# The last two tiles of a mixture-of-experts stage reach their tokens through PSUM

## The reference

```
gate_logits = einsum('bsd,de->bse', x, gate_kernel)          # 8 experts
top_k_weights, top_k_indices = top_k(gate_logits, 2)
top_k_weights = softmax(top_k_weights)
h0 = einsum('bsd,edm->bsem', x, w0)                           # 256 -> 512
h1 = einsum('bsd,edm->bsem', x, w1)
inter = silu(h0) * h1
out = einsum('bse,bsem,emd->bsd', combine, inter, wo)         # 512 -> 256
x = x + out
```

## Time and profile before

| | |
|---|---|
| median of 3 runs | 536.52 us (533.1 to 539.55) |
| profiled execution, its own time | 537.06 us |
| its span | 534.8 us |
| mean granted TensorE clock | 0.963 |
| busy in the span | PE 92%, DVE 64%, ACT 60%, POOL 25% |
| expert tiles in the span | about 404 to 519 us |
| after the last reduction | about 519 to 534.8 us |

### The profile page before, as it was taken

The page is one execution under the profiler, slowest core; times in us unless marked ns, Lnnn a source line. Parts: engine busy times, 40 slices in busy tenths (PEclk is TensorE's granted clock), DMA queues, the critical chain, the costliest instruction groups (busy, mean ns, idle before and its releaser), DMA issues. The chain is left out here.

```text
span 534.8 us, 11854 instructions
## 1 busy us (share of the span) xinstructions
PE 491.5 (92%) x4181; PEld 418.1 (78%) x4190; DVE 343.3 (64%) x743; ACT 318.4 (60%) x759; POOL 134.3 (25%) x150
## 2 busy tenths in 40 slices
PE   8899999999999999999999879999849999999970
PEld 3778888888898888888779857777637888888860
DVE  6666666667644676666558465678674667666754
ACT  4677777778526777777673267898313444544430
POOL 5710000012100000000000189996122433443220
PEclk9999999999999999999999997999859999999995
DMA  9521111211100112210000243441044555554527
GB/s 263 182 61 60 59 59 59 59 54 46 29 31 21 45 57 59 59 59 20 1 1 2 68 131 119 130 149 42 1 157 150 153 162 174 164 143 165 167 69 245
DMA packets 25043, 49.10 MB, mean 92 GB/s; under 512 B 2977, under 2 KB 12210, under 8 KB 25010
## 3 DMA queue, kind: packets, MB, share of 16 engines
q1 hardware_dynamic: 20434, 40.65, 25.0%
q0 software_dynamic: 2240, 6.04, 3.3%
q10 hardware_dynamic: 2336, 1.97, 1.2%
HBM read 42.48 MB, written 6.16 MB: 91 GB/s over the span
## 5 line engine op out<-in xcount | busy, mean ns | idle before, releaser
L717 PE MATMUL psum<-a_xt_hi,a_qk_hi 128*128 128x512 f32 x128 | 53.7, 420 | 0.9 <-POOL a_qk_lo L325 0.9
L629 DVE COPY a_weights_t<-psum 64x256 f32<-64x256 f32 x32 | 13.7, 428 | 60.7 <-PE psum L834 60.7
L717 PE MATMUL psum<-a_xt_hi,a_qk_lo 128*128 128x512 f32 x128 | 50.1, 392 | 0.0
L1066 ACT ACTIVATE x_probs<-psum,x_neg_max 128x128 f32<-128x128 f32 x128 | 45.8, 401 | 7.1 <-DVE x_neg_max L1124 7.1
L717 PE MATMUL psum<-a_xt_lo,a_qk_hi 128*128 128x512 f32 x128 | 50.0, 390 | 0.0
L1558 ACT ACTIVATE e_inner_hi<-psum 128x512 fp32r<-128x512 f32 x23 | 13.8, 598 | 56.4 <-PE psum L1734 56.4
L1002 POOL MEMSET x_v_pad<- 128x1024 f32 x1 | 1.0, 952 | 167.5 <-POOLq L262 167.5
L1723 PE MATMUL psum<-expert_w_hi,e_x_hi 128*128 x92 | 38.4, 418 | 1.2 <-ACT e_x_hi L1538 1.2
L1515 POOL DMA_INDIRECT picks_dram<-x_wout,e_pick_row x23 | 22.7, 987 | 62.6 <-DVE x_wout L1671 62.6
L1663 DVE TENSOR_TENSOR e_inner_lo<-psum,e_inner_hi 128x512 fp32r<-128x512 f32 x23 | 15.9, 692 | 34.6 <-ACT e_inner_hi L1558 34.6
L848 PE MATMUL psum<-a_weights_t,a_v 64*128 64x64 f32 x256 | 34.9, 276 | 3.5 <-issue 2.6
(11 more groups left out here) (235 smaller groups left out, 1497.6 us busy)
## 6 DMA issues: line engine op xcount, KB each, us to landing
x_k_t<-in_expert_wo SPq DMA_DIRECT2D x23, 512.0 KB, 3.8
a_qk_raw<-in_wqk SPq DMA_DIRECT2D x32, 256.0 KB, 2.6
x_xn_t<-in_expert_w SPq DMA_DIRECT2D x13, 512.0 KB, 3.8
a_wv_raw<-in_wv SPq DMA_DIRECT2D x17, 256.0 KB, 2.8
xn_dram<-xn SPq DMA_DIRECT2D x2, 1024.0 KB
x_probs_t<-in_expert_w SPq DMA_DIRECT2D x3, 512.0 KB, 3.8
x_sb<-in_x SPq DMA_DIRECT2D x2, 512.0 KB, 4.8
x_k_t<-in_wo SPq DMA_DIRECT2D x1, 1024.0 KB, 10.4
```

Source lines behind the costliest of these rows:

```text
L717: last = pe.matmul(out, pick_l(left[a], k), pick_r(right[b], k), start=start and n == 0, stop=n == 3 * KD - 1, skip_group_check=not start)
L1066: last = act.activation(probs[:, ch, place, :], s_ps[ch][:, place, :], ACT.Exp, bias=neg_max[:, ch, place:place + 1], accum_out=sums[:, b ...
```

## The change

Only tiles 0 to 20 are stored to `picks_dram` as before. Rows of tiles 21 and 22 (`LATE = 2`) stay in SBUF, scaled by their picks' shares, and are multiplied on PE with one-hot matrices that place each row at its token. For every batch b of 128 tokens one PSUM region `late_ps[b]` gathers tile 21's product, tile 22's product, and the rows of the first picks, scaled on ACT and added by a product with the identity. DVE adds the rows of the second picks to x by a multiply-add, and at the end the PSUM region.

What that needs beforehand: rows of `picks_dram` that tiles 21 and 22 would have written are filled with zeros (`clear_late`, POOL at tile 4). The shares are written to DRAM element by element (`store_shares`, SP at tile 1) and gathered by slot (`fetch_shares`, POOL at tile 5). The token of each late slot is worked out (`late_tokens`, POOL at tile 5), and the one-hot matrices are made by 8 compares each (`make_hot`, POOL at tiles 6 and 7). The result copies of tiles 20, 21 and 22 move from DVE to ACT (`last_rows`). Reads of `picks_dram` are issued by SP alone, in transfers of two batches, those of the second picks first; those of the first picks wait until the `wo` buffer they go into is free. Some routing tiles move into the unused `c.v`, which changes no instruction.

```diff
@@ constants
+LATE = 2
+STORED = TILES - LATE
+READ_ORDER = (4, 6, 0, 2)
+TOKEN_ORDER = (4, 5, 6, 7, 0, 1, 2, 3)
+AHEAD = 3
...
-    picked = [c.v, c.k_t[:, :, :].rearrange("p k n -> p (k n)").rearrange("p (b d) -> p b d", b=B)]
+    picked = [c.k_t[:, :, :].rearrange("p k n -> p (k n)").rearrange("p (b d) -> p b d", b=B), c.v]
+    hot = [row_hot[:, :, :].rearrange("p n r -> p (n r)").bitcast(F32), sb("e_late_hot", [P, B * P], F32)[:, :]]
+    hot = [t.rearrange("p (b t) -> p b t", b=B) for t in hot]
+    zeros = c.x_mask[:, :, :].rearrange("p a s -> p (a s)").bitcast(F32)
...
+    late_ps = [c.bank[i][:, h * D:(h + 1) * D] for i in (6, 7, 0, 3) for h in range(2)]
@@ SP
+                if left == TILES - 2:
+                    store_shares()
+            def store_shares():
+                sp.wait_ge(picks_known, 1)
+                sp.dma_start(share_dram[0:1, :], ones_f[0:1, 0:1]).then_inc(share_stored, 16)
+                sp.dma_start(share_dram[1:1 + PICKS * P, :].rearrange("(n p) d -> p n d", p=P),
+                             share[:, :, :].rearrange("p k b -> p (k b)").unsqueeze(2),
+                             allow_slow_non_contiguous=True).then_inc(share_stored, 16)
...
+            sp.wait_ge(late_cleared, 16 * LATE)
             for slot in range(2):
-                sp.wait_ge(y_stored[slot], 16 * ((TILES + 1 - slot) // 2))
-            for b in range(B):
-                sp.dma_start(picked[0][:, b, :], picks[0, :, b, :]).then_inc(gathered[b], 16)
-            for b in range(0, B, 2):
-                sp.wait_ge(mixed, TOPK * b + 3)
-                sp.dma_start(out[b], c.x_sb[:, b, :]).then_inc(out_stored, 16)
+                sp.wait_ge(y_stored[slot], 16 * ((STORED + 1 - slot) // 2))
+            for k in (1, 0):
+                for b in READ_ORDER:
+                    if k == 0:
+                        sp.wait_ge(wo_lo_ready, TILES if b < HB else TILES - 1)
+                    sp.dma_start(picked[k][:, b:b + 2, :], picks[k, :, b:b + 2, :]).then_inc(gathered[k][b // 2], 16)
+            for n in range(0, B, 2):
+                sp.wait_ge(finished, n + 1)
+                sp.dma_start(out[TOKEN_ORDER[n]], c.x_sb[:, TOKEN_ORDER[n], :]).then_inc(out_stored, 16)
@@ POOL
+            def clear_late():
+                pool.memset(zeros, 0.0).then_inc(zeroed, 1)
+                pool.wait_ge(zeroed, 1)
+                for tile in range(STORED, TILES):
+                    pool.indirect_dma_start(out=picks_dram, out_offset=bass.IndirectOffsetOnAxis(ap=pick_row[:, tile:tile + 1], axis=0),
+                                            in_=zeros, in_offset=None).then_inc(late_cleared, 16)
+            def fetch_shares():
+                pool.wait_ge(share_stored, 32)
+                for i in range(LATE):
+                    pool.indirect_dma_start(out=late_share[:, i:i + 1], out_offset=None, in_=share_dram,
+                                            in_offset=bass.IndirectOffsetOnAxis(ap=token_row[:, STORED + i:STORED + i + 1], axis=0)
+                                            ).then_inc(share_known, 16)
+            def late_tokens():
...
+            def make_hot(i):
+                for b in range(B):
+                    last = pool.tensor_scalar(hot[i][:, b, :], iota[:, 0:P], late_at[:, i, b:b + 1], None, ALU.is_equal)
+                last.then_inc(hot_made, 1)
...
                 if tile > 1:
                     store(tile - 2)
-            store(TILES - 2)
-            store(TILES - 1)
+                if tile == 4:
+                    clear_late()
+                elif tile == 5:
+                    fetch_shares()
+                    late_tokens()
+                elif 6 <= tile < 6 + LATE:
+                    make_hot(tile - 6)
@@ ACT
+                if not more(left, LATE + 1):
+                    last_rows(tile, slot, pair)
+            def last_rows(tile, slot, pair):
+                act.wait_ge(y_done, tile + 1)
+                act.wait_ge(y_stored[slot], pair * 16)
+                if tile < STORED:
+                    act.activation(y_rows[:, slot, :], y_ps[slot], ACT.Copy).then_inc(y_ready, 1)
+                else:
+                    act.wait_ge(share_known, 16 * LATE)
+                    at = tile - STORED
+                    act.activation(y_rows[:, slot, :], y_ps[slot], ACT.Copy, scale=late_share[:, at:at + 1]).then_inc(late_ready, 1)
...
-            for b in range(B):
-                act.dma_start(picked[1][:, b, :], picks[1, :, b, :]).then_inc(gathered[b], 16)
+            for n, b in enumerate(TOKEN_ORDER):
+                act.wait_ge(gathered[0][b // 2], 16)
+                act.activation(picked[0][:, b, :], picked[0][:, b, :], ACT.Copy, scale=share[:, 0, b:b + 1]).then_inc(scaled, 1)
@@ DVE
-                dve.wait_ge(y_done, tile + 1)
-                wait_past(dve, y_stored[slot], pair * 16)
-                dve.tensor_copy(y_rows[:, slot, :], y_ps[slot]).then_inc(y_ready, 1)
+                if more(left, LATE + 1):
+                    dve.wait_ge(y_done, tile + 1)
+                    wait_past(dve, y_stored[slot], pair * 16)
+                    dve.tensor_copy(y_rows[:, slot, :], y_ps[slot]).then_inc(y_ready, 1)
...
+            for b in TOKEN_ORDER:
+                dve.wait_ge(gathered[1][b // 2], 16)
+                dve.scalar_tensor_tensor(out=c.x_sb[:, b, :], in0=picked[1][:, b, :], scalar=share[:, 1, b:b + 1],
+                                         in1=c.x_sb[:, b, :], op0=ALU.mult, op1=ALU.add).then_inc(mixed, 1)
+            for n, b in enumerate(TOKEN_ORDER):
+                dve.wait_ge(mixed, n + 1)
+                dve.wait_ge(tokens_done, n // 2 * 2 + 2)
+                dve.tensor_tensor(c.x_sb[:, b, :], c.x_sb[:, b, :], late_ps[b], ALU.add).then_inc(finished, 1)
@@ PE
-                reduce(tile, slot, pair)
+                if left == 0:
+                    pe.wait_ge(late_ready, 1)
+                    pe.wait_ge(hot_made, LATE)
+                    for b in TOKEN_ORDER[:AHEAD]:
+                        to_tokens(b, 0)
+                reduce(tile, slot, pair, left)
+            def to_tokens(b, i):
+                pe.matmul(late_ps[b], hot[i][:, b, :], y_rows[:, (STORED + i) % 2, :], start=i == 0, stop=False, skip_group_check=True)
             tiles(pe, step)
+            for b in TOKEN_ORDER[AHEAD:]:
+                to_tokens(b, 0)
+            pe.wait_ge(late_ready, LATE)
+            for n, b in enumerate(TOKEN_ORDER):
+                to_tokens(b, 1)
+                pe.wait_ge(scaled, n + 1)
+                pe.matmul(late_ps[b], c.ident[:, :], picked[0][:, b, :], start=False, stop=True,
+                          skip_group_check=True).then_inc(tokens_done, 1)
```

More of the change, by code:

```diff
@@ L1368, with expert_phase @@
 TO_TILES = float(3 * P * 2 ** 22)
-def expert_phase(c, xn_dram, picks_dram, out):
+LATE = 2
[3 more added lines that the diff above has]
+AHEAD = 3
+def expert_phase(c, xn_dram, picks_dram, share_dram, out):
     nc = c.nc
@@ L1388, in expert_phase, with in_scratch @@
     chosen_id = sb("e_chosen_id", [P, B, TOPK], F32)
[L1389 removed]
+    scratch = c.v[:, :, :].rearrange("p b d -> p (b d)")
+    def in_scratch(at, n):
+        return scratch[:, at:at + n]
+    chosen = in_scratch(384, TOPK * B * NE).rearrange("p (k b e) -> p k b e", k=TOPK, b=B)
     either = sb("e_either", [P, B + 1, NE], BF16)
@@ L1398, in expert_phase @@
     base = sb("e_base", [P, NE], F32)
-    place = sb("e_place", [P, B, NE], F32)
-    place_k = sb("e_place_k", [P, TOPK, B, NE], F32)
+    place = in_scratch(576, B * NE).rearrange("p (b e) -> p b e", b=B)
+    place_k = in_scratch(640, TOPK * B * NE).rearrange("p (k b e) -> p k b e", k=TOPK, b=B)
     row_f = sb("e_row_f", [P, TOPK, B], F32)
-    reached = c.v[:, :, :].rearrange("p b d -> p (b d)")[:, 0:PICKS * TILES].rearrange("p (n t) -> p n t", n=PICKS)
+    reached = in_scratch(0, PICKS * TILES).rearrange("p (n t) -> p n t", n=PICKS)
     in_tile = sb("e_in_tile", [P, PICKS, TILES], F16)
@@ L1445, in expert_phase @@
     t_done, t_ready, t_lo_ready, y_done, y_ready = sem("e_t_done"), sem("e_t_ready"), sem("e_t_lo_ready"), sem("e_y_done"), sem("e_y_ready")
-    gathered = [sem(f"e_gathered{i}") for i in range(B)]
+    gathered = [[sem(f"e_gathered{k}_{b}") for b in range(0, B, 2)] for k in range(TOPK)]
     mixed, out_stored = sem("e_mixed"), sem("e_out_stored")
+    zeroed, late_cleared, late_chain, hot_made = sem("e_zeroed"), sem("e_late_cleared"), sem("e_late_chain"), sem("e_hot_made")
+    share_stored, share_known, late_ready = sem("e_share_stored"), sem("e_share_known"), sem("e_late_ready")
+    scaled, tokens_done, finished = sem("e_scaled"), sem("e_tokens_done"), sem("e_finished")
     def tiles(eng, step):
@@ L1516, in store @@
                                         in_=y_rows[:, slot, :], in_offset=None).then_inc(y_stored[slot], 16)
+            def clear_late():
[11 more added lines that the diff above has]
+            def late_tokens():
```

(20 more changed lines are left out.)

23 lines of the change are left out of this document (8 added, 15 removed).

## The result

The changed kernel is **slower by about 1.5%**. The first comparison gave 545.26 us against 538.86 for the kernel before on the same chip (ratio 1.0154, 95% interval 1.0118 to 1.019), a later one 545.05 against 537.35 (1.0171, 1.0113 to 1.0229); by the ratios that is 8.3 and 9.2 us. The prediction was 536.8, between 531.5 and 542.0, "the same" at 0.74. It was wrong.

What follows compares the result with a forecast made beforehand. TensorE was taken to bound the expert loop, a chain of waits the end. Tail -2.8, POOL's stall +2.0 and POOL beside VectorE +1.1 gave +0.3: 537.4 against 537.06, hence median 536.8 us, range 531.5 to 542.0.

Steps and rivals of the forecast that it cites:

- Share store on SP: 2048 four-byte packets ahead of tile 4's wo load on SP's queue: expected to cost nothing, upper end 3.4 us.
- cover of 5.35 us: Expert loop: lateness a POOL row load can have, beyond 3.6 us landing, before TensorE waits.
- Rival 4: Four-byte writes hold tile 4's weights: up to 3.4 us, replacing some of POOL's stall; 537.1 to 540.2 us; chance 0.06.
- the size of POOL's stall: TensorE's wait from POOL's added work at tiles 4 to 7: 3.1 us, bounds 0 and 9.7.
- load(10): POOL's row load for tile 10, behind both compare blocks: 7.4 us late, stopping TensorE for 2.0 us.
- load(9): POOL's row load for tile 9, behind the first eight compares, expected late through carried-over POOL work.
- 1.8 + 8c: Lateness of tile 9's row load: 1.8 us carried plus eight one-hot compares of c = 0.51 us each.
- the term for POOL beside VectorE: One-hot blocks meeting VectorE's wo_lo subtract lose 0.57 us a tile, 1.14 us for two.
- rival 3: VectorE's subtract and POOL's reads fully exclude each other: 2 x 1.23 us in place of 1.14; 538.1 us; chance 0.08.
- Rival 5: TensorE drops to clock 0.5 in the tail, costing 7.4 us: 544.2 us; chance 0.03.
- The tail: From tile 21's products to the end: TensorE's fp32 products at 0.442 us each set the pace; gain 2.8 us.
- The cover of 0.4 us for the first scaled rows: Tail: first-pick rows arrive some 0.4 us before TensorE's first pair needs them, so their reads were costed at nothing.

Runs made afterwards that it cites:

- either cure alone: Changed kernel with either the shares stored as 16 rows of 512 bytes (540.07 us, ratio 1.0065) or POOL's added work in smaller pieces (541.54 us, ratio 1.0081).

## Why the prediction was wrong

**The step that failed is "Share store on SP"**, in its sentence "I take 44 ns, the queue with the smaller packets: nothing; upper end 3.4". It priced the packets by their own time on the engines and looked for the harm in one place, the weights of tile 4. The packets were even cheaper than that, 9 ns. The cost came behind them: with 4-byte writes that share 64 bytes with their neighbours, the transfers under way (all of them touch DRAM) were slow for some 10 us, POOL's row loads among them, one of which landed 13.1 us after its issue in place of 3.6. By the prediction's cover of 5.35 us on top of 3.6 that is a stall of about 4; measured were 3.65 idle, and 3.9 us lost. Rival 4 named the same store, but with weights as the victim and at a price of 0 to 3.4; it also let POOL catch up meanwhile, so that its cost replaced the other stall. The two stalls lie four tiles apart and add up: either cure alone leaves 4.05 or 5.66 us of wait.

**The second step that failed is the size of POOL's stall:** 3.1 us were predicted, 4.55 idle and 6.9 lost. The mechanism was right, a load that POOL issues too late, but it came a load earlier than the sum has it. The sum puts the excess at load(10), behind sixteen compares, with load(9) late by 1.8 + 8c = 5.9 us, hardly more than the cover of 5.35. The run with the shares as 16 rows shows the lateness without the other stall: tile 6's load went out at 421.10, three steps of 4.87 later is 435.71, and load(9) went out at 445.19, 9.5 us late. That less 5.35 is 4.1; its wait was 4.05. While TensorE stood and then ran at half clock, POOL made the second eight compares, and tile 10 found its rows.

Two terms made most of the 3.6 us between 5.9 and 9.5. The compare was taken at 0.51 and took 0.59, 0.6 us for eight. And the term for POOL beside VectorE was too small: it counted the compares alone, at 0.57 a block, while in front of load(9) three of POOL's instructions met a subtract of wo_lo, and lost 0.9 (the second read of the shares), 0.7 (a store) and 0.7 us (a compare). The remaining 0.5 us lie in small operations and gaps. Full exclusion, rival 3 and the rule of the Trainium skill (SBUF — State Buffer, Who interferes with whom), is what these traces show: in every run each compare of more than 0.9 us, up to 1.69, overlapped a subtract and ended 0.38 to 0.48 us behind its end; where a compare went ahead, the subtract was longer (1.57 in place of 1.23 above). Only some 0.4 us at the seam overlapped freely. Rival 3 stood at 0.08, because the in_tile product's 1.72 us were read as a slowdown of less than half its overlap. VectorE's two compares beside it, taken one by one, read otherwise:

```profile
395.59 1.22 DVE L1618 TENSOR_TENSOR e_row_hot<-e_iota,e_at_row 128x1024 f16<-128x1024 f32 x1
...
396.73 1.83 DVE L1618 TENSOR_TENSOR e_row_hot<-e_iota,e_at_row 128x1024 f16<-128x1024 f32 x1
```

The product began at 395.75, within the first, and ended at 397.47, 0.66 us behind its end at 396.81; the second compare took 0.61 us longer than the first. Each of the two waited once for the other. Rival 3 priced the one-hot compares only, so its 1.3 us more are not what was lost here.

**A term was missing: the clock behind a stall.** The prediction counted a stall as its idle time. Behind the 4.55 us TensorE ran at 0.50 for 4.6 us, which made 6.85 of it. Rival 5 looked for the half clock in the tail, where it did not come.

**The tail was right:** 2.8 us predicted, 2.8 measured; 0.442 a product against 0.43. It was as predicted bound by TensorE, as the run without the identity products showed by gaining 1.6 us more there (15.7 to 14.1). The cover of 0.4 us for the first scaled rows, costed at nothing, was too thin in five of the ten other profiles, by 0.2 to 0.9 us.

**Sum:** -2.8 (predicted -2.8), +6.9 at tile 7 (predicted 3.1), +4.2 at tiles 2 and 3 (predicted 0; 0.4 of it at tile 2, where the runs with spaced writes lose as much), +0.6 ahead of tile 0 (predicted 0): +8.9 against +0.3. Either of the two stalls alone would have left the time within the range of 531.5 to 542.0, as the runs with one cure did (540.07 and 541.54); it took both.

## What to carry to other kernels

Price a small scattered transfer by what it does to its neighbours, not by its own packets: look at the GB/s and the time of one ordinary packet in the microseconds behind it. Where single values must go to DRAM one by one, give each its own 64 bytes, or turn them in SBUF into rows first. And work squeezed in front of a prefetch should be cut into pieces no larger than what the issuing engine idles per tile (2.6 us here), since what exceeds it is carried to the next prefetch; count in what that engine loses beside another. A stall in a dense loop costs its idle time and then, if the clock falls, here about half as much again.

## What the hardware showed

- Behind 2048 writes of 4 bytes to DRAM, sixteen to the same 64 bytes, the transfers of this kernel, all to or from DRAM, were slow for about 10 us after the packets were through (4 KB packets 0.16 to 1.7 us); behind writes 64 or 512 bytes apart they were not, nor behind copies from SBUF to SBUF. With 1024 of them the stretch was hardly shorter (422 to 431 us). Why, whether the writes to one place queue up in the memory, is not shown.
- A wait of 3.65 us left the clock at 1.00 in one profile, one of 3.5 in another profile of the same kernel was followed by 0.50; 4.55 us was followed by 0.50 too.
- POOL's compare of 128 columns with a scalar from SBUF takes 0.59 us. Where one met VectorE's subtract with two SBUF inputs (1.23 us) by more than some 0.4 us, one of the two waited for the other: the compare took up to 1.69, the subtract up to 1.63. POOL's indirect transfers, about 1.0 us to issue, took up to 2.06 beside it.
